# Feature-crossing recommender on one core: the last tile of 128 samples taken out of its group of four and run by itself, its rows turned by the tensor engine

## What is computed

```python
embed = tables[arange(26)[None, :], sparse_inputs]      # 2048 samples x 26 fields x 32 numbers
p = einsum('bfe,bge->bfg', embed, embed)                # all products of two fields
l_z = einsum('bfe,feh->bh', embed, w_z)                 # h = 256
l_p = einsum('bfg,fgh->bh', p, w_p)
l_1 = relu(concatenate([l_z + l_p + l_b, dense_inputs], axis=-1))
h = relu(l_1 @ W1 + b1)                                 # 128
y = sigmoid(h @ Wf + bf)                                # 1 score of a sample
```

## Time and profile before

| | |
|---|---|
| time, median of 3 runs | 600.0 us (599.43 to 600.08) |
| span of the profiled execution | 548.8 us |
| that median less the span | 51.2 us |
| busy: POOL, DVE | 409.0 us (75%), 417.5 us (76%) |
| busy: ACT, PE | 139.7 us (25%), 131.1 us (24%) |
| indirect DMAs on POOL | 416, first issued at 3.6 us, last at 522.5 us |
| from the end of the last issue to the end of the span | 25.3 us |

### The profile page before, as it was taken

One profiled execution on the slowest core, in us unless ns is written; L12 is line 12 of the kernel. 1 busy time (PEld: TensorE's weight loads), 2 busy tenths in 40 slices (PEclk: granted clock), 3 DMA queues, 4 the chain that ended last, 5 costly groups with the idle time before them and its releaser, 6 DMA issues.

```text
span 548.8 us, 1701 instructions
## 1 busy us (share of the span) xinstructions
PE 131.1 (24%) x204; PEld 48.0 (9%) x204; DVE 417.5 (76%) x250; ACT 139.7 (25%) x333; POOL 409.0 (75%) x430
## 2 busy tenths in 40 slices
PE   0000000415334100060465100051433600005067
PEld 0000000201111000020121000020110100002023
DVE  4204199998992369998996419999899547999995
ACT  0000004404551021704452010340455110250323
POOL 6777777777777777777777777777777777777792
PEclk9999999976567555585666655567665555558569
DMA  6222323122122222222112222222112222312220
GB/s 148 21 14 13 13 13 14 13 13 14 14 13 13 13 13 14 13 14 13 13 14 14 13 13 13 13 14 13 14 13 13 14 14 13 14 13 13 13 46 2
DMA packets 19640, 9.56 MB, mean 17 GB/s; under 512 B 9888, under 2 KB 19629, under 8 KB 19629
## 3 DMA queue, kind: packets, MB, share of 16 engines
q0 software_dynamic: 13312, 6.84, 22.4%
q1 hardware_dynamic: 6318, 2.63, 2.1%
HBM read 8.85 MB, written 0.01 MB: 16 GB/s over the span
## 4 chain that ended last, share of the span: by engine, by line
POOL 69%; issue 23%; DVE 6%; DMA 1%; PE 1%; ACT 0%; ACTq 0%; POOLq 0%; DVEq 0%
POOL rows L286 66%; DVE pairs L368 3%; DVE prod L348 2%; POOL prod L302 2%; POOL prod L313 1%; DMA rows<-in_L_rec_tables,which 1%; PE ps_h L643 0%; DMA raw<-in_r_sparse_inputs 0%; DVE pair_rows L404 0%; PE ps_h L680 0%; ACT scores L551 0%; PE ps_copy L692 0%; ACT hidden L537 0%; ACTq L120 0%; DVE pairs_T L395 0%
## 5 line engine op out<-in xcount | busy, mean ns | idle before, releaser
L286 POOL DMA_INDIRECT rows<-in_L_rec_tables,which x416 | 393.5, 946 | 128.4 <-issue 125.8
L348 DVE TENSOR_TENSOR prod<-ps_copy,rows 128x1664 f32<-128x1664 f32 (+12 forms) x103 | 194.2, 1910 | 16.8 <-ACT ps_copy L471 16.8
L368 DVE TENSOR_REDUCE pairs<-prod 128x76 f32<-128x2432 f32 (+13 forms) x73 | 195.3, 2680 | 0.0
L626 PE MATMUL ps_h<-field_rows,wz 128*128 128x512 f32 x96 | 59.4, 784 | 290.3 <-ACT field_rows L482 285.4
L379 DVE STREAM_TRANSPOSE rows_T<-rows 128x512 f32<-128x512 f32 (+1 forms) x28 | 18.6, 663 | 98.1 <-DMA rows<-in_L_rec_tables,which 90.7
L471 ACT COPY ps_copy<-rows 128x128 f32<-128x128 f32 (+2 forms) x63 | 21.2, 336 | 273.3 <-DMA rows<-in_L_rec_tables,which 273.0
L643 PE MATMUL ps_h<-pair_rows,w_pair 96*128 96x512 f32 (+2 forms) x64 | 50.2, 943 | 100.3 <-ACT pair_rows L505 84.4
L482 ACT COPY field_rows<-rows_T 32x512 f32<-32x512 f32 (+1 forms) x112 | 58.7, 524 | 34.9 <-DVE rows_T L379 33.4
L626 PEld LDWEIGHTS ps_h<-field_rows,wz 128*128 128x128 f32 x96 | 23.8, 258 | 328.0 <-issue 292.1
L505 ACT COPY pair_rows<-pairs_T 32x256 f32<-32x256 f32 (+1 forms) x96 | 33.5, 349 | 63.1 <-DVE pairs_T L391 61.9
L643 PEld LDWEIGHTS ps_h<-pair_rows,w_pair 96*128 96x128 f32 (+2 forms) x64 | 17.7, 296 | 130.4 <-ACT pair_rows L505 71.9
(11 more groups left out here) (37 smaller groups left out, 31.7 us busy)
## 6 DMA issues: line engine op xcount, KB each, us to landing
rows<-in_L_rec_tables,which POOLq DMA_INDIRECT x416, 3.4
wz<-in_L_rec_w_z SPq DMA_DIRECT2D x1, 768.0 KB, 5.8
field_rows<-rows_T SPq DMA_DIRECT2D x16, 32.0 KB, 1.9
w_pair<-in_w_low SPq DMA_DIRECT2D x1, 288.0 KB, 5.4
w_back<-in_w_high SPq DMA_DIRECT2D x1, 288.0 KB, 5.7
raw<-in_r_sparse_inputs SPq DMA_DIRECT2D x1, 156.0 KB, 2.2
w<-in_L_rec_W SPq DMA_DIRECT2D x1, 128.0 KB
dense_in<-in_r_dense_inputs SPq DMA_DIRECT2D x1, 104.0 KB, 3.2
```

The lines of the kernel that those rows point to most:

```text
L286: nc.gpsimd.indirect_dma_start(rows[:, r % 2, f, k, :], None, table_rows, bass.IndirectOffsetOnAxis(ap=which[:, t, f:f + 1], axis=0),).the ...
L348: ins = nc.vector.tensor_tensor(products(r, s)[:, 0:tiles, at:at + g + 1, :], own.broadcast_to([P, tiles, g + 1, E]), rows[:, r % 2, 0:g + ...
L368: nc.vector.tensor_reduce(pairs[:, 0:tiles, first:end], products(r, s)[:, 0:tiles, :, :], AX.X, ALU.add)\
L626: ins = nc.tensor.matmul(ps_h0[:, h, :], wz[:, j, h * P:(h + 1) * P], field_rows[:, j, :, :, :].rearrange("p q t b -> p (q t b)"), start=( ...
```

## The change

The 16 tiles go in six phases: three groups of four as before, then tiles 12 and 13 (phase 3), tile 14 (phase 4) and tile 15 (phase 5, `END`). Products and sums are made phase by phase. Tiles 12 to 14 are transposed, laid out and summed on PE together, as a group of three and 384 wide; their rows are transposed on DVE during phase 4. Tile 15 has buffers of its own inside the free half of `rows` (`solo_rows`, `solo_pairs`, `pool_prod`). Its rows and sums are transposed by PE against an identity into the fourth buffer of `ps_copy` (`turn_solo`), copied to `solo_T` by ACT (`lay_solo`) and multiplied 128 wide (`sum_solo`), in eleven turns; each turn waits for the copy of the one before, since there is one buffer. It then has its own layers, 128 wide. POOL takes 8 pairs of field 24 and 12 of field 25 of tile 15 alone.

In all groups ACT no longer lays rows out for the first six chunks. SP writes each chunk to a tensor in DRAM with four DMAs (`passage`), waits for them, and reads it back in the layout of `field_rows` with one. Fields go in coarser units and stages, most by two; the pair blocks are laid out all three together at a group's end; and the sums and layers of a group stand in one run on PE.

```diff
+PHASES = GROUPS + 2
+PLAIN = [(0, 4), (4, 8), (8, 12)] + [(f, f + 2) for f in range(12, 26, 2)]
+ENDING = [(0, 4), (4, 8), (8, 12)] + [(f, f + 2) for f in range(12, 22, 2)] + [(f, f + 1) for f in range(22, 26)]
+UNITS = [PLAIN] * (PHASES - 1) + [ENDING]
+STAGES = [[(0, 4), (4, 8), (8, 10)] + [(f, f + 2) for f in range(10, 24, 2)] + [(24, 25), (25, 26)]] * (GROUPS - 1)\
+    + [PLAIN] * (PHASES - GROUPS) + [ENDING]
...
+    TILE_RANGE = [(0, K)] * (ROUNDS - 1) + [(0, 2), (2, K - 1), (K - 1, K)]
+    ABREAST = [K] * (ROUNDS - 1) + [K - 1]
+    TURNS = [("rows", 0), ("rows", 1), ("rows", 2), ("rows", 3), ("pairs", 0), ("rows", 4), ("pairs", 1),
+             ("rows", 5), ("rows", 6), ("pairs", 2), ("pairs", 3)]
...
             # sync
-            sp.wait_ge(rows_turned, CH * r + end)
-            sp.wait_ge(lz_summed, MOVED * (r - 1) + end)
-            for q in range(QUADS):
-                for u in range(PER):
-                    sp.dma_start(field_rows[Q * u:Q * (u + 1), first:end, q, :, :].rearrange("p c k b -> p c (k b)"),
...
+            for r in range(ROUNDS):
+                n = ABREAST[r]
+                for j in range(MOVED):
+                    sp.wait_ge(rows_turned, CH * r + j + 1)
+                    if r:
+                        sp.wait_ge(rows_in[j], DMA * r)
+                    for q in range(QUADS):
+                        sp.dma_start(passage[j, :, :, q, 0:n * Q].rearrange("u e x -> e u x"),
+                                     rows_T[Q * q:Q * (q + 1), j, :, 0:n, :].rearrange("p u k b -> p u (k b)"))\
+                            .then_inc(passed[j], DMA)
+                    if r:
+                        sp.wait_ge(lz_summed, MOVED * (r - 1) + j + 1)
+                    sp.wait_ge(passed[j], DMA * QUADS * (r + 1))
+                    sp.dma_start(field_rows[:, j, :, 0:n, :].rearrange("p q k b -> p q (k b)"),
+                                 passage[j, :, :, :, 0:n * Q].rearrange("u e q x -> (u e) q x")).then_inc(rows_in[j], DMA)
...
             # scalar, phase END
+            for u, (first, end) in enumerate(UNITS[END]):
+                copy_fields(END, u)
                 if first == 0:
+                    for v in range(PLACES):
+                        lay_pairs(r, v)
                 if first == 4:
+                    lay_solo("rows", 0)
+                    lay_last_rows(r)
+                    lay_last_pairs(r)
                 if first == 8:
+                    lay_solo("rows", 1)
+                    make_hidden0(r)
+                if first == 14:
+                    lay_solo("rows", 2)
+                    make_hidden1(r)
+                if first == 16:
+                    make_scores(r)
...
+            def turn_solo(what, c):
...
+                nc.tensor.transpose(ps_copy_bank(SOLO_COPIES)[0:wide, 0:P], came, ident[:, :]).then_inc(solo_turned, 1)
...
             # tensor, the last group
+            for j in range(MOVED):
+                sum_lz(r, j)
+            sum_dense(r)
+            turn_solo("rows", 0)
+            for c in range(BLOCKS):
+                sum_lp(r, c)
+            turn_solo("rows", 1)
+            sum_lp(r, TAIL)
+            turn_solo("rows", 2)
+            sum_h1(r)
```

More of the change, by code:

```diff
@@ new lines, in add_up @@
+            def add_up(p, s):
+                n = STAGES_BEFORE[p] + s
+                first, end = stage_range(p, s)
+                low, high = TILE_RANGE[p]
+                dve.wait_ge(multiplied, n + 1)
+                if 0 < p < ROUNDS and s == 0:
+                    dve.wait_ge(pairs_turned, NPM * p)
+                    dve.wait_ge(tail_turned, p)
+                into = solo_pairs[:, :, first:end] if p == END else pairs[:, low:high, first:end]
+                nc.vector.tensor_reduce(into, products(p, s), AX.X, ALU.add).then_inc(summed, 1)
@@ L458, in _ @@
+                        for m in range(NPM if group_ends else 0):
+                            if stage_of(p, last_field(m)) == s - 1:
+                                turn_pairs(p, m)
+                if group_ends:
+                    lay_tail(r)
+            make_solo_half()
         @block.scalar
         def _(act):
[L460 to L472 removed]
@@ L601, in _ @@
-            make_hidden1(ROUNDS - 1)
-            for p in range(HALVES):
-                make_scores_part(p)
+                    lay_solo("rows", 1)
+                    make_hidden0(r)
+                if first == 14:
+                    lay_solo("rows", 2)
+                    make_hidden1(r)
+                if first == 16:
+                    make_scores(r)
+                if first == 18:
+                    lay_solo("rows", 3)
+                    lay_solo("pairs", 0)
+                if first == 22:
+                    lay_solo("rows", 4)
+                    lay_solo("pairs", 1)
@@ new lines, in sum_solo @@
+            def sum_solo(what, c):
+                n = TURNS.index((what, c))
+                pe.wait_ge(solo_laid, n + 1)
+                if n == 0:
+                    pe.wait_ge(hidden0_made, HALVES * ROUNDS)
+                last = what == "pairs" and c == TAIL
+                if what == "rows":
+                    weights, came = wz[:, c, :], solo_T[:, n, :]
+                elif last:
+                    weights, came = w_pair[:, TAIL, :], solo_T[:, TURNS.index(("rows", MOVED)), :]
+                else:
+                    weights, came = w_pair[0:block_rows(c), c, :], solo_T[0:block_rows(c), n, :]
+                for h in range(HALVES):
+                    ins = nc.tensor.matmul(ps_h0[:, h, 0:P], weights[:, h * P:(h + 1) * P], came, start=(n == 0), stop=last)
+                    if last:
+                        ins.then_inc(half_summed, 1)
```

585 lines of the change are left out of this document (291 added, 294 removed).

## The result

The changed kernel takes **617.66 us** (617.55 to 617.96, 4 runs), the kernel before in the same job 599.71 us (598.93 to 600.08, 4 runs): ratio 1.0303, 95% interval 1.0288 to 1.0318. The forecast was 596.3 with a range of 591 to 603. Sign and size were wrong.

A forecast was written before the change was run, and what follows sets the result against it. It took POOL's gathers, 416 at 1.25 us ending at 523.5, as the bound, with only the 25.3 us after them to shorten. DVE's end at 538.8 plus 6.3 gave 545.1, with 51.2 around it 596.3 us; range 591.0 to 603.0.

The forecast's parts named there:

- With 51.2 around it: 596.3 us: Whole kernel: 51.2 us taken to lie around the predicted span of 545.1, giving a time of 596.3 us.
- when PE lets ACT go for the second turned copy and the activations: Start of tile 15: PE's sums and pair blocks release ACT, so DVE goes on with fields 12 on at 518.9.
- POOL: 0 us: POOL's gathers: the change adds nothing, POOL has to stop for nothing and the last issue stays put.
- last issue 523.5: POOL: 416 gathers, one each 1.25 us, the last issue ending at 523.5 us as before.
- a gap over 0.3 us: Sign on POOL: any gap between gathers over 0.3 us would undo the first step, on what bounds the kernel.
- DVE comes to tile 15 at 505.3: DVE in phases 3 and 4: 5.2 us more work, in cover of the gathers; it reaches tile 15 at 505.3.
- SP's path, 5.05 us a chunk: SP's writes and reads through DRAM: 5.05 us a chunk, chunks queue, sixth read begins at 504.2, rows arrive at 507.1.
- Rival (3): Slower DRAM path, reads over 5.6 apart; at +1 us a chunk 601.5 to 603; 0.22 with rival (2) and everything slower.
- ACT waits behind `lay_solo`, DVE stops for 7 and 1.2 us: Start of tile 15: ACT waits for PE, so DVE stops nearly 7 us before fields 8 to 11, later 1.2.
- From the last sum to the end, 6.3: After DVE's last sum: transpose, copy, matmuls, layers and store take 6.3 us, against 9.5 before.
- rival (2): PE stays at 1.2 GHz through the pair blocks: 601.9 us; chance 0.22 with Rival (3) and all that is slower.
- rival (1): Chunks pass SP faster, DVE's two stops shrink to 2 us, span 539.7, time 590.9 us; chance 0.18.

The follow-up runs named there:

- e1: Changed kernel without the round trip through DRAM, ACT laying out the rows of the group of three too, where before takes 551 us: 544.82 us, ratio 0.991.
- e2: Kernel before with only SP's path through DRAM added, in groups 0 to 2, in place of ACT's copies: 550.71 us, ratio 0.9997.
- e10: Changed kernel with SP's path overlapped, a chunk's four writes issued ahead of the read of the chunk before: 617.2 us, ratio 1.0313 to before.
- e14: Changed kernel with ACT's turned rows and activations in tile 15 moved behind the copies for DVE: 610.28 us, 1.019 of before.
- e13: Kernel before with 32 small spare ACT copies added in group 0: 610.14 us, ratio 1.0198.
- e6: Changed kernel without the round trip through DRAM, rows laid out by ACT, where before takes about 600 us: 632.62 us, ratio 1.0567 to before.
- e16: Changed kernel with the changes of e10 and e14 both: 613.95 us, ratio 1.023 to before.
- e0: Kernel before, unchanged, profiled once more: 550.87 us, span 548.7.
- e4: Kernel before, unchanged, profiled on the chip of the comparison where it takes about 600 us: 598.4 us, span 596.2.
- e17_more_matmuls: Kernel before with ten of the last group's matmuls cut in two, 256 columns each in place of 512: 551.24 us, ratio 1.0009.

## Why the prediction failed

**The step that failed** is the one that joined trace and times: "With 51.2 around it: 596.3 us". The 51.2 us were not around the span. They were inside it, as 1.40 in place of 1.25 us a gather from some 214 us on (37.5 us to the last gather) and as a tail of 35.2 in place of 25.3, in executions of another condition; around the span lie 2.1, and the rest is what the jobs differ by (598.4 and 600.0). A launch cost of 51 us should have been doubted: nothing in the rows supported it, and each duration that I took into the sum was one of the 551 condition.

In the sum itself the step that failed is when PE lets ACT go for the second turned copy and the activations, so that DVE gets fields 12 on. DVE was to go on at 518.9, 4.6 us ahead of the end of the gathers; it went on at 588.7, 27.3 us behind it. From there on the sum held: DVE's last work took 19.9 us (put at 19.9), the layers 7.0 (6.3).

Point by point:

- *POOL: 0 us.* Right as a difference: 561.4 and 561.0. "Gathers every 1.25" and "last issue 523.5" do not hold in the condition that was timed, and I had named a gap over 0.3 us as what would undo the step.
- *DVE comes to tile 15 at 505.3*, 18.2 us ahead of the end of the gathers. It came there at 561.2, 0.2 us ahead. In e1, which has the same work on DVE and met the 551 condition, it came at 505.31, so the working was right for that condition, one slip of 0.5 us aside: six chunks and a half of 384 columns are 3.5 us by the row used, not 3.0. In the other, "issue" stands between DVE's rows: 121.1 us ahead of L400 in all.
- *SP's path, 5.05 us a chunk.* Near 5.3 in the 551 condition (e2), about 10 in the 600 condition: 5.60 for four issues (put at 2.6). DVE's transposes of the six chunks came within 5 us of where the sum had them, counted from the end of the gathers (509.7 to 534.6); the sixth read was put 19.3 us ahead of that end and was issued 2.6 behind it. This is the term whose size was off most, by 22 us. Rival (3) named "reads more than 5.6 apart" as its mark. The mark came, the mechanism is not the one that rival (3) had, a slower landing: it is SP's issues. And e10 shows that the sixth chunk may come later still at no cost as long as ACT waits for the second turned copy.
- *ACT waits behind `lay_solo`, DVE stops for 7 and 1.2 us.* The mechanism is right, place by place. The sizes were 8.2 and 11.9 us. The second was mis-sized by 10.7 us; e14 shows that some 7 us come back with another order.
- *From the last sum to the end, 6.3.* 7.0 (608.5 to 615.5), and 6.9 in e1 in the 551 condition, so this term was 0.6 short in both. PE ran at 1.2 GHz there (granted 0.50 from 600 to 613), which answers to the 0.4 us that rival (2) put on its last matmuls and to longer passes of 128 columns. Its main price, 3.9 us in the pair blocks, was half paid: their first six passes came 0.64 us apart, as at 1.2 GHz, the other six mostly 0.32 apart (granted 0.72 from 569 to 577). In e1 they were 0.32 apart and the clock was granted 1.00 (506 to 510).
- *No rival* had what decided: that an engine could be short of instructions to issue. Rivals (2) and (3) gave 602 to 603 on this side.

The sum itself, span 545.1, was never tried: no run of the changed kernel met the 551 condition. What e1 shows there supports its frame (rival (1)'s span within 1.2 us), and e2 its time for a chunk in groups 0 to 2; whether six chunks in a row pass at that pace was not seen there.

**What is shown and what is not.** Shown: in the 600 condition instructions, not their length, are what an engine pays with (e13: 32 copies of 0.2 us at 68 us cost 11.7 us); the loss lies behind the last gather; taking SP's path out and giving its work to ACT does not cure it (e6); ACT's order is 7 of the 18 us (e14). What SP's path costs in the last group is not isolated: nothing for 6 us more with ACT's order as it was (e10), about 3 us with e14's order (e16). Argued only: that PE's 24 matmuls in 12 us from 565.2 on are why its signal stands until 587. Against a simple count speaks that from 588 to 613 PE did 63 matmuls with no such spacing, so either PE's matmuls are not counted like the others or the limit had ended by then. Open too is where the condition comes from. Loads of program code are not it, as far as the traces show: before has nine of them in either condition (e0 and e4, after the start, 8 KB each, and one of 16 KB), and in e13 none stands between 38.2 and 116.9 us, where the copies were spaced. One candidate is the recording itself, since every timed execution was recorded. In the 600 condition the records of before have no landing for the moves that the earlier trace rows put at 1.9 us, and waits are put down to "issue" or "remote". Counted in the traces, events are in fact missing: before, e0_before_again and e17_more_matmuls, in the 551 condition, hold 7,202 landings of DMAs each, e4_before_third holds 979 for the same DMAs. All five traces of the 551 condition have 6,882 to 8,642, all fifteen of the 600 condition 927 to 1,213; from 40 to 500 us that is 26 in 20 us in e4 and 256 in before. So condition and lost records go together without an exception. Which of the two brings the other, or whether a third thing brings both, no run here tells. The Trainium skill, "NOTIFIC — the notification-queue block" (section 7.1), says that this block's inner pipeline always holds its producers up rather than lose a record, and that this can throttle an engine. Held-up engines would fit; the lost events are not what that sentence describes. No run here shows the block or a run without records, so this is a fit and not a finding.

## What to carry to other kernels

When a profile's span and the times differ by more than a few microseconds, find out why before any sum is made; a pace taken from one (here one gather in 1.25 us) may not hold in the other. If a kernel may run where instructions are short, count them per engine and stretch, and hand work over in few long ones; ask of what stands in cover of one engine whether another waits behind it (32 copies in cover of POOL made DVE 20 us late); a version with more short instructions can win 0.9% in one condition and lose 5.7% in the other. In an in-order queue put what waits for a slow partner behind what feeds the bottleneck: that alone was worth 6.9 us here.

## What the hardware showed that I had not expected

The same chip ran the same kernel in 598.5 us (19 runs in two jobs) and in 550.8 us (13 runs in a third), each within 0.3%. In the slower condition ACT ran 19 short instructions in 1.96 us and the next ones 1.40 us apart, 70 us after the start. Later the same step is seen on each of four engines: ACT copies of 0.27 to 0.30 us (452 to 460 in e4), transposes of DVE (0.27 us, 1.40 apart near 556 in the changed kernel), DMA issues of SP (four in 5.60) and gathers of POOL (mean 1.40 from 232 us on). And the traces of that condition lack six of seven of the landings of DMAs that the other condition records (979 for 7,202).
